# First batch's normalisation split over three engines, key weights split on POOL, and the second projection walked chunk by chunk

## The chip, the cores and the metric

The kernel runs on one core of a Trainium2 chip. Its engines are TensorE (PE), VectorE (DVE), ScalarE (ACT), GpSimd (POOL) and SyncE (SP, which here only issues DMA). Time is the device time of one execution in microseconds; lower is better. Before the change three runs gave a median of 674.53 us (673.94 to 674.96).

## What is computed

Two transformer-like layers on x of shape (2, 512, 512). Only the start matters here: the layer norm of x and the first projections.

```python
xn = _layernorm(x, axis=-1)                 # (x - mean) / sqrt(var + 1e-5), per row of 512
qkv = xn @ w_qkv                            # 512 -> 32 query heads, 8 key heads, 8 value heads of 16
xq, xk = _apply_rope(q), _apply_rope(k)     # products with cos and sin tables, then sums
x = x + attention(xq, xk, xv) @ w_o + ffn0(xn)
xn = _layernorm(x, axis=-1)
x = x + attn1(xn) + ffn1(xn)
```

## The kernel before

Everything is one program with an instruction order written by hand for each engine; semaphores join them. There is no scheduler. The change touches the first stage, `qkv_stage`, which takes about the first 50 us.

The 1024 rows of x are 8 tiles of 128 rows, four for each batch. `Norm` does a tile in steps: `dve_stats` (L88, L90: mean and variance), `act_std` (L94: square root on ACT), `dve_norm` (L98 reciprocal, L100 subtract and multiply, in place), `pe_transpose` (L108, four 128x128 transposes into a bank of PSUM), `act_hi` (L117, rounds the transposed tile to fp32r, the high part) and `dve_lo` (L122, the rest, the low part). Every product is three matmuls, high by high, low by high and high by low (`three_pass`, L52 to L54), so weights are split in the same way: `wqkv_hi` by ACT (L565 for the 128 key columns of all four chunks at once, L577 for the other 640 columns chunk by chunk) and `wqkv_lo` by POOL (L528 keys, L531 chunks 0 to 2) and DVE (L629, chunk 3).

The order on PE: 14 products of the identity matrix (L696) that compute nothing that is kept, the first batch's four tiles with a few more identity products between them (`IDENTITY_PRODUCTS`), then `pair(0)` (keys of the first batch, 12 matmuls), `pair(1)` (24 matmuls), the transposes of the second batch's four tiles (L108 x16), and `pair(2)`. Before `pair(n)` with n of 2 or more PE waits until DVE has made the four rope products (L647) of pair n - 2, because they read the bank that pair n overwrites. So `pair(2)` waits for the products of `pair(0)`.

The order on DVE: the first batch's stats and norms, its four low parts, the second batch's four stats (they wait for the one DMA that loads the second batch), the low part of weight chunk 3, the second batch's four norms, then the products of `pair(0)` and `pair(1)`.

All loads of this stage are issued by SP on one queue, in the order ident, four x tiles, four weight chunks, second batch of x, cos, sin, lr_raw, mask, first feed-forward weights.

## Time and profile before

| | |
|---|---|
| median of three runs | 674.53 us (673.94 to 674.96) |
| the profiled execution, its time | 674.68 us |
| its span in the trace | 672.9 us |
| PE busy | 663.8 us (99%) |
| DVE, ACT, POOL busy | 418.2 (62%), 294.3 (44%), 241.3 us (36%) |

The profiled execution took 1.8 us more than its span, which lies around it. PE is busy in nearly the whole span, so a change can move the end only where PE waits, or where PE does work that could be left out.

### The profile page before, as it was taken

The page shows a single profiled execution, that of the slowest core. Times are in us where ns is not written, and L with a number is a line of the kernel's source. Part 1 is how long each engine was busy: PE and PEld are TensorE (multiplying, and loading weights), DVE is VectorE, ACT ScalarE, POOL GpSimd, SP SyncE. Part 2 cuts the span into 40 slices and gives each one's busy share as a digit, 9 for nine tenths or more (in the row PEclk, how much of TensorE's full clock was granted, in tenths as well). Part 3 has the DMA queues.
Part 4 walks back from the last instruction along what each step waited for, and adds up shares of the span by engine and source line. Part 5 has one row for each costly group of instructions (what it writes and reads, how often), then busy time and mean ns, then how long its engine had stood idle before and what let it go on. Part 6 is the DMA issues. An engine that isn't in the chain of part 4 may idle for free.

```text
span 672.9 us, 9999 instructions
## 1 busy us (share of the span) xinstructions
PE 663.8 (99%) x3518; PEld 505.2 (75%) x3518; DVE 418.2 (62%) x987; ACT 294.3 (44%) x558; POOL 241.3 (36%) x242
## 2 busy tenths in 40 slices
PE   8999999999999999999999999999999999999998
PEld 7786666666666666666787778888888888888886
DVE  6957867766777677665366655377555665646501
ACT  4324555455554555455434425344433444343321
POOL 3595233133222322222234636703232242323443
PEclk9999999999999999999999999999999999999999
DMA  9448334352223322121155520500010011112011
GB/s 292 136 145 185 99 78 109 78 129 78 78 58 89 77 80 65 50 79 49 48 162 161 176 91 1 159 1 32 32 32 33 32 63 32 32 32 78 1 63 62
DMA packets 23145, 55.17 MB, mean 82 GB/s; under 512 B 3732, under 2 KB 4088, under 8 KB 22040
## 3 DMA queue, kind: packets, MB, share of 16 engines
q1 hardware_dynamic: 22840, 54.41, 27.9%
q8 instruction: 28, 0.46, 0.3%
q14 instruction: 21, 0.17, 0.1%
q10 hardware_dynamic: 256, 0.13, 0.1%
HBM read 42.86 MB, written 11.54 MB: 81 GB/s over the span
## 4 chain that ended last, share of the span: by engine, by line
PE 91%; POOL 2%; issue 1%; DVE 1%; DMA 1%; ACT 1%; SPq 1%; ACTq 0%; DVEq 0%
PE bank L52 25%; PE bank L54 23%; PE bank L53 23%; PE bank L1085 6%; PE bank L1120 5%; PE bank L1107 3%; PE bank L180 2%; PE bank L696 1%; PE bank L1093 1%; PE bank L108 1%; PE bank L344 1%; POOL wqkv_lo L531 1%; DMA k_stack<-k_hi 1%; PE bank L1677 1%; DMA q_lo<-rope_lo 1%
## 5 line engine op out<-in xcount | busy, mean ns | idle before, releaser
L1031 DVE CUSTOM_DVE_ANT_0 bank<-bank,mask 128x512 f32<-128x512 f32 (+3 forms) x256 | 118.4, 523 | 57.3 <-PE bank L1085 57.0
L217 POOL TENSOR_TENSOR up_w_lo<-up_w_eff,up_w_hi 128x512 fp32r<-128x512 f32 x50 | 66.8, 1342 | 98.5 <-ACT up_w_hi L213 98.5
L382 POOL TENSOR_TENSOR down_h_lo<-hidden,down_h_hi 128x512 fp32r<-128x512 f32 x50 | 66.2, 1324 | 88.3 <-ACT down_h_hi L377 88.3
L983 ACT ACTIVATE probs<-bank 128x512 f32<-128x512 f32 x160 | 85.0, 598 | 27.6 <-PE bank L1107 24.9
L52 PE MATMUL bank<-x0T_hi,up_w_hi 128*128 128x512 f32 x224 | 95.7, 427 | 0.0
L54 PE MATMUL bank<-x0T_lo,up_w_hi 128*128 128x512 f32 x224 | 88.5, 395 | 0.0
L53 PE MATMUL bank<-x0T_hi,up_w_lo 128*128 128x512 f32 x224 | 88.3, 394 | 0.0
L944 POOL TENSOR_SCALAR_AFFINE_SELECT probs<-probs 128x512 f32<-128x512 f32 x64 | 39.9, 635 | 120.0 <-ACT probs L983 120.0
L52 PE MATMUL bank<-down_w_hi,down_h_hi 128*128 128x512 f32 x200 | 78.5, 392 | 0.4 <-DVE bind_cols L1397 0.4
L53 PE MATMUL bank<-down_w_hi,down_h_lo 128*128 128x512 f32 x200 | 78.0, 390 | 0.0
L377 ACT ACTIVATE down_h_hi<-hidden 128x512 fp32r<-128x512 f32 x50 | 31.6, 631 | 91.3 <-PE bank L54 91.3
L52 PEld LDWEIGHTS bank<-x0T_hi,up_w_hi 128*128 128x128 f32 x224 | 42.0, 187 | 23.4 <-issue 16.5
L1085 PE MATMUL bank<-k_stack,q_stack 48*128 48x512 f32 (+3 forms) x256 | 56.8, 341 | 0.7 <-DMA k_stack<-k_hi 0.7
L1107 PE MATMUL bank<-q_stack,k_stack 49*128 49x512 f32 x160 | 57.0, 443 | 0.0
L284 DVE SCALAR_TENSOR_TENSOR up_gated<-up_tanh,bank 128x512 f32<-128x512 f32 x50 | 34.2, 684 | 32.2 <-ACT up_tanh L277 31.8
L290 DVE SCALAR_TENSOR_TENSOR hidden<-up_gated,bank 128x512 f32<-128x512 f32 x50 | 34.3, 685 | 30.5 <-PE bank L54 30.3
L213 ACT ACTIVATE up_w_hi<-up_w_eff 128x512 fp32r<-128x512 f32 x50 | 31.1, 631 | 47.4 <-DVE up_w_eff L204 47.4
L54 PEld LDWEIGHTS bank<-x0T_lo,up_w_hi 128*128 128x128 f32 x224 | 42.1, 188 | 10.2
L1085 PEld LDWEIGHTS bank<-k_stack,q_stack 48*128 48x128 f32 x256 | 35.7, 185 | 18.1 <-issue 16.3
L53 PEld LDWEIGHTS bank<-x0T_hi,up_w_lo 128*128 128x128 f32 x224 | 42.2, 188 | 6.0
L52 PEld LDWEIGHTS bank<-down_w_hi,down_h_hi 128*128 128x128 f32 x200 | 37.6, 188 | 8.2 <-DVE bind_cols L1397 0.5
L54 PE MATMUL bank<-down_w_lo,down_h_hi 128*128 128x512 f32 x112 | 43.7, 390 | 0.0
(167 smaller groups left out, 1361.2 us busy)
## 6 DMA issues: line engine op xcount, KB each, us to landing
w_raw<-in_w_gate_up SPq DMA_DIRECT2D x25, 512.0 KB, 3.4
w_raw<-in_w_down SPq DMA_DIRECT2D x25, 256.0 KB, 3.6
q_stack<-q_hi SPq DMA_DIRECT2D x32, 128.0 KB, 3.3
att<-att_T SPq DMA_DIRECT2D x16, 256.0 KB, 2.0
q_hi<-rope_hi SPq DMA_DIRECT2D x8, 256.0 KB
q_lo<-rope_lo SPq DMA_DIRECT2D x8, 256.0 KB
q_stack<-q_lo SPq DMA_DIRECT2D x16, 128.0 KB, 3.6
attention_or_xn<-att SPq DMA_DIRECT2D x16, 128.0 KB
```

What stands on the lines that cost most here:

```text
L52: pe.matmul(out, w_hi, m_hi, start=first, stop=False, skip_group_check=True)
L53: pe.matmul(out, w_lo, m_hi, start=False, stop=False, skip_group_check=True)
L54: return pe.matmul(out, w_hi, m_lo, start=False, stop=last, skip_group_check=True)
L217: pool.tensor_tensor(self.half(self.w_lo[:, o % 2], k), self.half(self.w_eff, k), f32(self.half(self.w_hi[:, o % 2], k)), ALU.subtract).th ...
L284: dve.scalar_tensor_tensor(out=self.ut[:, b, :], in0=self.th[:, b, :], scalar=1.0, in1=self.product_bank(o, b, 0)[:, :], op0=ALU.add, op1= ...
L290: dve.scalar_tensor_tensor(out=self.hid[:, o, b * S:(b + 1) * S], in0=self.ut[:, b, :], scalar=0.5, in1=self.product_bank(o, b, 1)[:, :], ...
L382: pool.tensor_tensor(self.h_lo[:, k % 2, :], self.hid[:, o, b * S:(b + 1) * S], f32(self.h_hi[:, k % 2, :]), ALU.subtract).then_inc(self.h ...
L944: pool.affine_select(out=diag, in_=diag, compare_op=ALU.is_ge, fill=0.0, base=0, pattern=[[0, REP], [1, P]], channel_multiplier=-1).then_i ...
L983: act.activation(pt[:, BLOCK_OF[KEY_PIECES[p]], :, :], narrow.bank(("keys", g, p))[:, :].rearrange("p (h s) -> p h s", h=REP), ACT.Exp).th ...
L1031: dve.tensor_tensor_reduce(out=own, in0=own, in1=e.mask[:, S - w:S], scale=1.0, scalar=NEG, op0=ALU.add, op1=ALU.max, accum_out=rmax[:, i, ...
L1085: last = pe.matmul(bank[:, n * w:(n + 1) * w], qst[K, slot, h + n, i * P:(i + 1) * P], kst[K, slot, 0:w], start=(n == 0), stop=(n == nh - ...
L1107: pe.matmul(narrow.bank(("keys", g, p))[:, :], kst[K, slot, j * P:(j + 1) * P], qst[K, slot, :, i * P:(i + 1) * P], start=True, stop=True) ...
```

## The change

1. Loads: ident is issued by ACT, ahead of its other work, instead of by SP. The key columns of all weights come as one DMA (256 KB in rows of 512 bytes), the other 640 columns as four. cos and sin are issued ahead of the second batch of x.
2. The first batch's norm: tile 0 by POOL, tiles 1 and 3 by ACT (as x * rstd + shift, where DVE makes the 128x1 shift = -mean * rstd), tile 2 by DVE.
3. Key weights: POOL makes both high and low part; ACT's L565 goes away.
4. DVE does the low part of weight chunk 3 ahead of the second batch's stats instead of behind them.
5. `pair(1)` goes chunk by chunk over both its halves, instead of half by half.
6. Identity products: 10 instead of 14 at the start, and 2, 2, 2, 5 behind the tiles instead of 2, 3, 2, 7.

```diff
         def sync(sp):
-            sp.dma_start(e.ident[:, :], d["ident"]).then_inc(e.ident_in, 16)
             for t in range(NJ):
                 sp.dma_start(x_sb[:, t, :], d["x"][t * P:(t + 1) * P, :]).then_inc(x_loaded[t], 16)
+            sp.dma_start(w_raw[:, :, 0:P], d["w_qkv"][:, 0:P].rearrange("(c p) n -> p c n", p=P)).then_inc(w_loaded[0], 16)
             for c in range(NC):
-                sp.dma_start(w_raw[:, c, :], d["w_qkv"][c * P:(c + 1) * P, :]).then_inc(w_loaded[c], 16)
-            sp.dma_start(x_sb[:, NJ:, :], d["x"][S:].rearrange("(t p) n -> p t n", p=P)).then_inc(x_loaded[NJ], 16)
+                sp.dma_start(w_raw[:, c, P:], d["w_qkv"][c * P:(c + 1) * P, P:]).then_inc(w_loaded[1], 16)
             sp.dma_start(cos[:, :], d["cos"]).then_inc(consts, 16)
             sp.dma_start(sin[:, :], d["sin"]).then_inc(consts, 16)
+            sp.dma_start(x_sb[:, NJ:, :], d["x"][S:].rearrange("(t p) n -> p t n", p=P)).then_inc(x_loaded[NJ], 16)
...
-            pool.wait_ge(w_hi_ready, 1)
-            pool.tensor_tensor(w_lo[:, :, 0:P], w_raw[:, :, 0:P], f32(w_hi[:, :, 0:P]), ALU.subtract).then_inc(w_lo_ready, 1)
+            pool.wait_ge(norm.rst, 1)
+            pool.tensor_scalar(x_sb[:, 0, :], x_sb[:, 0, :], norm.mv[:, 0, 0:1], norm.rstd[:, 0:1],
+                               ALU.subtract, ALU.mult).then_inc(by_pool, 1)
+            pool.wait_ge(w_loaded[0], 16)
+            pool.tensor_copy(w_hi[:, :, 0:P], w_raw[:, :, 0:P]).then_inc(by_pool, 1)
+            pool.wait_ge(by_pool, 2)
+            pool.tensor_tensor(w_lo[:, :, 0:P], w_raw[:, :, 0:P], f32(w_hi[:, :, 0:P]), ALU.subtract).then_inc(by_pool, 1)
...
+            def normalise(t):
+                act.wait_ge(shifted, 1 + t // 2)
+                act.activation(x_sb[:, t, :], x_sb[:, t, :], ACT.Identity, bias=shift[:, t:t + 1],
+                               scale=norm.rstd[:, t:t + 1]).then_inc(act_normed, 1)
+
+            act.dma_start(e.ident[:, :], d["ident"]).then_inc(e.ident_in, 16)
             norm.act_std(act, 0)
             norm.act_std(act, 1)
             norm.act_std(act, 2)
+            normalise(1)
+            norm.act_std(act, 3)
             norm.act_hi(act, 0)
-            norm.act_std(act, 3)
+            normalise(3)
             norm.act_hi(act, 1)
             norm.act_hi(act, 2)
-            split_keys()
             norm.act_hi(act, 3)
+            act.wait_ge(w_loaded[1], 16 * NC)
             for c in range(NC):
                 act.activation(w_hi[:, c, P:], w_raw[:, c, P:], ACT.Copy).then_inc(w_hi_ready, 1)
...
             for t in range(NJ):
                 norm.dve_lo(dve, t)
+            dve.wait_ge(w_hi_ready, NC)
+            dve.tensor_tensor(w_lo[:, NC - 1, P:], w_raw[:, NC - 1, P:], f32(w_hi[:, NC - 1, P:]), ALU.subtract).then_inc(w_lo_last, 1)
             for t in range(NJ, NT):
                 norm.dve_stats(dve, t)
-            dve.wait_ge(w_hi_ready, NC + 1)
-            dve.tensor_tensor(w_lo[:, NC - 1, P:], w_raw[:, NC - 1, P:], f32(w_hi[:, NC - 1, P:]), ALU.subtract).then_inc(w_lo_last, 1)
...
-                for r in range(1 if k == 0 else 2):
+                halves = range(1 if k == 0 else 2)
+                for c, r in ((c, r) for c in range(NC) for r in halves) if n == 1 else ((c, r) for r in halves for c in range(NC)):
...
-            identity_products(14)
+            identity_products(10)
```

On DVE, the piece between the first batch's low parts (L122) and the products of pair 0 (L647 before, L673 now). Before:

```order
L122 TENSOR_TENSOR x0T_lo<-bank,x0T_hi 128x4x128 x4
L88 BN_STATS norm_stats<-x 128x6
L90 BN_AGGR norm_mv<-norm_stats 128x2
...
L629 TENSOR_TENSOR wqkv_lo<-wqkv_raw,wqkv_hi 128x640
L98 RECIPROCAL norm_rstd<-norm_std 128x1
L100 TENSOR_SCALAR x<-x,norm_mv,norm_rstd 128x512
```

And now:

```order
L122 TENSOR_TENSOR x0T_lo<-bank,x0T_hi 128x4x128 x4
L653 TENSOR_TENSOR wqkv_lo<-wqkv_raw,wqkv_hi 128x640
L88 BN_STATS norm_stats<-x 128x6
L90 BN_AGGR norm_mv<-norm_stats 128x2
...
L98 RECIPROCAL norm_rstd<-norm_std 128x1
L100 TENSOR_SCALAR x<-x,norm_mv,norm_rstd 128x512
```

The weight chunk moved from behind the second batch's four stats to ahead of them; the stats, norms and products behind it are the same instructions in the same order.

On SP, the queue of loads at the start of the program. Before:

```order
L487 DMA ident<-in_ident 128x128
L489 DMA x<-in_x 128x512 x4
L491 DMA wqkv_raw<-in_w_qkv 128x768 x4
L492 DMA x<-in_x 128x4x512
L493 DMA cos<-in_cos 128x512
L494 DMA sin<-in_sin 128x512
L495 DMA lr_raw<-in_lr 96x4096
```

And now:

```order
L492 DMA x<-in_x 128x512 x4
L493 DMA wqkv_raw<-in_w_qkv 128x4x128
L495 DMA wqkv_raw<-in_w_qkv 128x640 x4
L496 DMA cos<-in_cos 128x512
L497 DMA sin<-in_sin 128x512
L498 DMA x<-in_x 128x4x512
L499 DMA lr_raw<-in_lr 96x4096
```

The second batch of x (128x4x512) is now the last load ahead of lr_raw, where sin was; ident has left this queue.

## Rows read from the trace of the kernel before

**Rows 1.** Waits of PE, whole span: us in total, times, longest.
```profile
PE bank L1085 <- DMA k_stack<-k_hi: 0.7, 1, 0.7
```

**Rows 2.** Timeline of DVE, 4 to 24.4: start us, us, instruction, idle before.
```profile
5.92 0.13 DVE L98 RECIPROCAL norm_rstd<-norm_std 128x1 f32<-128x1 f32 x1
...
14.42 0.69 DVE L88 BATCH_NORM_STATS2 norm_stats<-x 128x6 f32<-128x512 f32 x1 [0.81 <-DMA x<-in_x]
...
17.63 1.38 DVE L629 TENSOR_TENSOR wqkv_lo<-wqkv_raw,wqkv_hi 128x640 fp32r<-128x640 f32 x1
18.93 0.15 DVE L98 RECIPROCAL norm_rstd<-norm_std 128x1 f32<-128x1 f32 x1
...
21.55 0.67 DVE L647 SCALAR_TENSOR_TENSOR rope_products<-bank,cos 64x512 f32<-64x512 f32 x1
...
23.69 0.69 DVE L647 SCALAR_TENSOR_TENSOR rope_products<-bank,cos 64x512 f32<-64x512 f32 x1
```

**Rows 3.** Timeline of PE, 12.6 to 24.6.
```profile
13.89 0.47 PE L52 MATMUL bank<-x0T_hi,wqkv_hi 128*128 128x512 f32 x1 [0.20 <-POOL wqkv_lo L528]
...
22.69 1.91 PE L108 MATMUL bank<-ident,x 128*128 128x128 f32 x16
24.44 0.49 PE L52 MATMUL bank<-x0T_hi,wqkv_hi 128*128 128x512 f32 x1
```

**Rows 4.** Timeline of SP, 0 to 9.2: its DMA issues.
```profile
0.81 0.39 SPq L487 DMA_DIRECT2D ident<-in_ident  x1
...
5.04 0.81 SPq L492 DMA_DIRECT2D x<-in_x  x1
...
7.11 0.44 SPq L494 DMA_DIRECT2D sin<-in_sin  x1
```

**Rows 5.** DMA by short windows: size, us from issue to landing; packets moved, 2.0 to 2.5.
```profile
DMA packets 104, 0.06 MB, mean 112 GB/s; under 512 B 16, under 2 KB 97, under 8 KB 104
...
wqkv_raw<-in_w_qkv SPq DMA_DIRECT2D x1, 384.0 KB, 6.7
...
x<-in_x SPq DMA_DIRECT2D x1, 1024.0 KB, 9.4
...
sin<-in_sin SPq DMA_DIRECT2D x1, 256.0 KB, 9.5
```

**Rows 6.** Timeline of ACT, 4 to 19.
```profile
12.29 0.59 ACT L117 ACTIVATE x0T_hi<-bank 128x512 fp32r<-128x512 f32 x1
12.77 2.61 ACT L577 ACTIVATE wqkv_hi<-wqkv_raw 128x640 fp32r<-128x640 f32 x4
```

**Rows 7.** Timeline of POOL, 0.7 to 19.
```profile
12.47 1.27 POOL L528 TENSOR_TENSOR wqkv_lo<-wqkv_raw,wqkv_hi 128x512 fp32r<-128x512 f32 x1 [9.83 <-ACT wqkv_hi L565]
13.71 4.62 POOL L531 TENSOR_TENSOR wqkv_lo<-wqkv_raw,wqkv_hi 128x640 fp32r<-128x640 f32 x3
```

**Rows 8.** Timelines of POOL and DVE, 46 to 52.
```profile
46.22 2.56 POOL L217 TENSOR_TENSOR up_w_lo<-up_w_eff,up_w_hi 128x512 fp32r<-128x512 f32 x2
48.73 2.28 POOL L547 TENSOR_TENSOR rope_sum<-rope_products 128x512 f32<-128x512 f32 x1
...
47.65 2.21 DVE L638 TENSOR_TENSOR rope_lo<-rope_sum,rope_hi 128x1024 fp32r<-128x1024 f32 x1
```

**Rows 9.** Groups of POOL by form: busy us, mean ns, idle before.
```profile
L944 POOL TENSOR_SCALAR_AFFINE_SELECT probs<-probs 128x512 f32<-128x512 f32 x64 | 39.9, 635 | 120.0 <-ACT probs L983 120.0
```

**Rows 10.** Timeline of PE, 2 to 12 (x4 is one tile's transposes).
```profile
2.68 6.13 PE L696 MATMUL bank<-ident 128*128 128x128 f32 x28 [2.68 <-DMA ident<-in_ident]
8.65 0.60 PE L108 MATMUL bank<-ident,x 128*128 128x128 f32 x4
...
9.54 0.60 PE L108 MATMUL bank<-ident,x 128*128 128x128 f32 x4
...
11.53 0.60 PE L108 MATMUL bank<-ident,x 128*128 128x128 f32 x4
```

**Rows 11.** Windows at the end: PE busy first, PEclk is the granted clock.
```profile
669.00:672.90 3.90, 0.73 (x4) 0.27 (x2) 1.45 (x3) 0.00 (x0) 0.00 (x0) 1.00 0.73 269
```

More of the change, by code:

```diff
@@ L465, in qkv_stage @@
                     e.xT_hi, e.xT_lo)
-        w_loaded = [sem(f"wqkv_loaded{c}") for c in range(NC)]
+        w_loaded = [sem("wqkv_keys_loaded"), sem("wqkv_rest_loaded")]
         consts = sem("rope_tables_loaded")
@@ L469, in qkv_stage @@
         lr_lo, products, stored = e.lr0_lo, e.rope_products, e.rope_stored
-        w_hi_ready, w_lo_ready, w_lo_last = sem("wqkv_hi_ready"), sem("wqkv_lo_ready"), sem("wqkv_lo_last_ready")
+        shift = sb("norm_shift", [P, NJ])
+        shifted, act_normed, by_pool = sem("norm_shift_ready"), sem("normed_by_act"), sem("tile0_normed_keys_hi_keys_lo_wqkv_lo")
+        norm.normed_in_order = {0: (by_pool, 1), 1: (act_normed, 1), 3: (act_normed, 2),
+                                **{t: (norm.normed, t - 2) for t in range(NJ, NT)}, 2: (norm.normed, 1)}
+        w_hi_ready, w_lo_last = sem("wqkv_hi_ready"), sem("wqkv_lo_last_ready")
         v_mm, v_rows, v_ones = sem("v_mm"), sem("v_rows_copied"), sem("v_ones")
@@ L561, in scalar @@
         def scalar(act):
-            def split_keys():
-                for c in range(NC):
-                    act.wait_ge(w_loaded[c], 16)
-                act.activation(w_hi[:, :, 0:P], w_raw[:, :, 0:P], ACT.Copy).then_inc(w_hi_ready, 1)
+            def normalise(t):
[3 more added lines that the diff above has]
+            act.dma_start(e.ident[:, :], d["ident"]).then_inc(e.ident_in, 16)
             norm.act_std(act, 0)
@@ L618, in vector, with reciprocal, shift_of @@
         def vector(dve):
-            norm.dve_stats(dve, 0)
-            for t in range(1, NJ):
-                norm.dve_stats(dve, t)
-                norm.dve_norm(dve, t - 1)
-            norm.dve_norm(dve, NJ - 1)
+            def reciprocal(t):
+                dve.wait_ge(norm.stdd, t + 1)
+                dve.reciprocal(norm.rstd[:, t:t + 1], norm.std[:, t:t + 1]).then_inc(norm.rst, 1)
+            def shift_of(t):
+                dve.wait_ge(norm.rst, t + 1)
+                dve.tensor_scalar(shift[:, t:t + 1], norm.mv[:, t, 0:1], norm.rstd[:, t:t + 1], -1.0,
+                                  ALU.mult, ALU.mult).then_inc(shifted, 1)
+            norm.dve_stats(dve, 0)
+            norm.dve_stats(dve, 1)
+            reciprocal(0)
+            norm.dve_stats(dve, 2)
+            reciprocal(1)
+            shift_of(1)
+            norm.dve_stats(dve, 3)
+            norm.dve_norm(dve, 2)
+            reciprocal(3)
+            shift_of(3)
             for t in range(NJ):
                 norm.dve_lo(dve, t)
+            dve.wait_ge(w_hi_ready, NC)
+            dve.tensor_tensor(w_lo[:, NC - 1, P:], w_raw[:, NC - 1, P:], f32(w_hi[:, NC - 1, P:]), ALU.subtract).then_inc(w_lo_last, 1)
             for t in range(NJ, NT):
                 norm.dve_stats(dve, t)
-            dve.wait_ge(w_hi_ready, NC + 1)
-            dve.tensor_tensor(w_lo[:, NC - 1, P:], w_raw[:, NC - 1, P:], f32(w_hi[:, NC - 1, P:]), ALU.subtract).then_inc(w_lo_last, 1)
             for t in range(NJ, NT):
```

27 lines of the change are left out of this document (13 added, 14 removed).

## The prediction

> **What bounds the kernel now.** PE is busy in 99% of the span (table above), so I first read PE's waits over the whole span: behind the start, no wait on a load or a store is longer than 0.7 us [rows 1]. A time won or lost in the first stage, at the point where PE goes over to unbroken work, should then reach the end whole, because everything behind hangs on PE's own order. That point is `pair(2)`. So the question is when PE can start it, and I read the timelines of the engines up to there.
>
> PE starts `pair(0)` at 13.89, its second-batch transposes at 22.69 and `pair(2)` at 24.44 [rows 3]. The transposes, 16 of them and two records each, end their issue at about 24.4. DVE ends the fourth product of `pair(0)`, for which `pair(2)` waits, at 23.69 + 0.69 = 24.38 [rows 2]. The two paths arrive together: no wait shows, but DVE's path has no slack at all. This is the thing to see before any sum is made: a faster PE alone wins nothing here.
>
> DVE's path begins at 14.42, when the second batch of x has landed: stats to 17.63, the low part of weight chunk 3 to 18.93, norms to 21.55, products to 24.38 [rows 2]. Without the weight chunk that is 3.21 + 5.45 = 8.66 us from the first stats to the end of the fourth product.
>
> **PE's side, part by part.** The 14 identity products and the tile behind them are spaced (8.65 - 2.68) / 28 = 0.213 us a record; behind that a tile with its two identity products, 8 records, takes 9.54 - 8.65 = 0.89 us, 0.11 a record [rows 10]. That is the lower and the higher of the two clock levels (1.2 and 2.4 GHz), and the rise came at the end of this unbroken work. With ten products, tile 0 can be transposed at 2.68 + 20 x 0.213 = 6.94, tile 1 at 6.94 + 8 x 0.213 = 8.65 (still the lower level), tiles 2 and 3 at 9.54 and 10.43, ended at 11.03. Before, tile 3 started at 11.53 [rows 10] and its high part on ACT, behind the key weights, at 12.29 [rows 6]. Now ACT can start it at 11.06, 1.23 earlier. `pair(0)` came 13.89 - 12.29 = 1.60 behind it and should come at 12.66.
>
> For this the four norms must be ready in time. POOL's tensor_scalar is not in the trace of before. The nearest row with one input is 0.635 us for 128x512 [rows 9], one with two inputs 1.27 [rows 7]; I take the first, for the kind, and both are covered: the reciprocal of tile 0 ended at 5.92 + 0.13 = 6.05 before [rows 2] and should end near 5.7, with ident's 0.39 of issue gone from SP's queue [rows 4]; so POOL is done at 6.4 to 7.0 against 6.94. ACT's normalisation I price by its 128x512 pass, 0.59 [rows 6]: two of them, and both stand where ACT waited for PE. DVE loses three norms of 0.55 and gains two 128x1 operations; it is not late there. POOL's copy and subtraction for the keys, 0.6 to 1.3 plus 1.27, end near 10 and are hidden until 12.66.
>
> `pair(0)` and `pair(1)` are 36 matmuls at 0.233, 8.4 us, if nothing stops them. Before they took 22.69 - 13.89 = 8.8, as PE waited 0.4 for POOL's third chunk. The new order asks for chunk 2 only after 12 matmuls of `pair(1)`, near 18.3, and POOL has it by 17.7 (below). So PE is through at 21.1 instead of 22.69, 1.6 us earlier. If PE alone counted, this would be the gain.
>
> **DVE's side.** ACT starts the high parts of the other weights 12.77 - 12.29 = 0.48 behind tile 3 [rows 6], now at 11.54, and ends them 2.61 later, at 14.15. The last weight load, issued some 0.47 ahead of the 5.04 of the next, landed 6.7 later, at 11.27 [rows 4, 5], so this holds if it is no later. DVE then asks for the low part of chunk 3 at 14.2. POOL is at its own three chunks by then, 4.62 / 3 = 1.54 each [rows 7], at 12.3 to 13.9, to 15.4, to 16.95. Here the rows show a clash. Before, DVE's L629 took 1.38 from 17.63 [rows 2] while POOL's last chunk ran until 18.33 [rows 7]; 19.01 - 18.33 leaves 0.68 for the work itself. Again DVE's L638, asked at 47.65, ended at 49.86, 1.13 behind the end of POOL's second L217 at 48.73, and POOL's next instruction took 2.28 instead of 1.27 [rows 8]. Two-input work in SBUF on the two engines takes turns by instruction. So DVE does chunk 3 at 15.4 to 16.1, and POOL's third chunk is 0.7 later, at 17.65. DVE's next step can't start before 16.07.
>
> The Trainium skill has this as a rule (SBUF — State Buffer, Who interferes with whom): a DVE instruction with two SBUF inputs and a GpSimd instruction that reads SBUF share one port pair, and the second blocks until the first has ended. By that rule the trace agrees; without it the bound would be 14.2 + 0.7 = 14.9.
>
> Then the load. The second batch of x landed at 5.04 + 9.4 = 14.44, with cos and sin behind it; sin landed at 7.11 + 9.5 = 16.61 [rows 4, 5]. Now cos and sin are ahead, and the second batch stands where sin stood, with the same bytes in front of it. It should land when sin did, 16.61, less about 0.3 since ident (0.39 of issue [rows 4]) runs beside the queue, plus about 0.25 for the key columns in 512-byte rows. That last number is my choice between nothing and 2 us: from 2.0 to 2.5 us, where ident's small rows moved, the queue made 112 GB/s, at which 256 KB would take 2.3 us [rows 5], but that stretch is mostly the start of the first transfer. I take 16.55.
>
> DVE's stats start at the later of 16.07 and 16.55. The products of `pair(0)` end at 16.55 + 8.66 = 25.21, and `pair(2)` starts at 25.27 instead of 24.44. The last norm ends at 22.5, so the transposes are over by 23.0 and PE then stands still for over 2 us. The 1.6 us won on PE are given back in that wait, and 0.83 more is lost.
>
> **Sum.** Pair 2 later by 0.83, the rest unchanged in order and length: by the profiled execution 674.68 + 0.83 = 675.5; the median of the runs shown is 0.15 lower, so 675.4 for the median. All edits on PE, POOL and ACT are worth nothing of their own here; their cover is DVE's path, and if that were gone they would give 1.6.
>
> **Rivals.**
> - *The load isn't late.* cos and sin are a quarter of the bytes of this stretch, and sin may have been slow through lr_raw's large rows beside it. Between the last weights (11.27) and the second batch (14.44) the queue moved 1 MB in 3.17 us [rows 5]; by that rate 512 KB more put the second batch 1.58 later, less 0.05 as above, at 15.97. Then DVE's turn behind POOL decides (16.07): 24.73 + 0.06, +0.35, or +0.2 to -0.3 if the turns fall better. 674.2 to 674.9. 17 in 100.
> - *PE decides after all*: DVE's path is short enough, and the gain is the 1.6 to 1.75 us of PE: 672.8 to 673.0. It needs stats at 14.9 or earlier. Against it: DVE can't have chunk 3 before ACT's 14.15, and the 8.66 us behind. 5 in 100.
> - *Small rows cost more*: the queue behind the key columns is 0.6 to 2 us later. Over 0.5 more, the loss passes 1.35; 676.0 to 677.5. 8 in 100.
> - *POOL isn't ready for early work.* Before, POOL did nothing for 9.83 us ahead of its first arithmetic at 12.47 [rows 7], so nothing shows that it could work at 5.7. If it starts only at t, PE waits at tile 0 for t + 0.64, and as it is idle from 6.94, it is likely at its lower clock again behind. From t = 7 on, each us comes into ACT's 11.54 and from there into DVE's. For a price I take t = 9, halfway between 5.7 and 12.47: tile 0 at 9.65, 2.7 later than in my sum, the weights' high parts at 14.2, DVE's stats 4.5 behind them at 18.7, `pair(2)` at 27.4: +3.0, 677.5; with a low clock for all four tiles up to 679. 15 in 100.
> - *The clock falls in PE's 2 us wait.* At the lower level a matmul takes 0.2 us more, and some 8 of them cost 1.7: 677. Against it: in the last 3.9 us PE did 0.73 us of work and the granted clock stayed 1.00 [rows 11]. 5 in 100.
>
> The GPSIMD Engine Reference of the Trainium skill (2.1, Instruction dispatch) says that the first call of a freshly loaded GpSimd kernel also pays for loading its code, about 6 us. Counted from the end of POOL's memsets at 12.47 - 9.83 = 2.64 that would be a start at 8.6 and 677.1, an estimate by that page. No run here shows it.
>
> **How the numbers follow.** My forecast has the remaining 50 in 100, 675.4, its own range 674.9 to 675.9. About 0.2%, 1.35 us, is what a measurement of this kernel can tell from no change. Faster: only the PE rival, 0.05. Slower: small rows, POOL and clock, 0.28. Same: 0.67. The range leaves out the PE rival below, and the worse half of POOL's and of the clock's above: 673.9 to 677.1.
>
> **What would show it.** Right: the first stats of the second batch start at 16 to 17 us; PE starts `pair(0)` near 12.7, ends `pair(1)` near 21, and waits over 1.5 us for DVE's products ahead of `pair(2)` at 25.3; DVE's weight chunk (L653) takes over 1.2 us, with POOL's end as its releaser in time; POOL's tensor_scalar starts near 5.7. Wrong: stats at 15, or `pair(2)` right behind the transposes; a POOL instruction that starts at 8 or later, with PE idle from 7. What makes the prediction wrong most easily is the landing of the second batch, on which the whole sum hangs one for one.

## The result and the profile after

The changed kernel takes 676.83 us (median of 14 executions, 675.25 to 678.49), the kernel before 674.74 us in the same comparison (14 executions, 673.94 to 675.89). The ratio is 1.003, with a 95% interval of 1.0019 to 1.004: slower, by 2.1 us or 0.3%. The forecast was 675.4 us, in a range of 673.9 to 677.1.

The 14 times of the changed kernel don't lie around their median. They fall into two groups, and the mean granted clock of PE over the whole span, which is kept for each execution, parts them exactly:

| mean granted clock | executions | times |
|---|---|---|
| 0.999 to 1.000 | 7 | 675.25 to 676.23, median 675.77 |
| 0.997 | 7 | 677.42 to 678.49, median 677.72 |

The forecast of 675.4 is close to the first group. The second group is 1.95 us longer, all of it lies above the top of the range (677.1), and the profiled execution (677.42 us, span 675.7 us) is one of it. All 78 executions of the kernel before that stood beside the experiments have 0.999 or 1.000. One of these 78 took 677.45 us all the same, so a long time alone is no sign of a lower clock.

The page of the profiled execution, parts 1 and 2, shows this only in one digit. PE is still busy in 98% of the span, and the clock has an 8 in the second of the 40 slices (16.9 to 33.8 us), where the page of the kernel before has a 9:

```profile
PE 663.2 (98%) x3504; PEld 505.0 (75%) x3504; DVE 417.7 (62%) x986; ACT 295.4 (44%) x559; POOL 244.7 (36%) x244
...
PEclk9899999999999999999999999999999999999999
```

The waits of PE in this execution (us in total, times, longest) show a new one, 1.9 us for DVE's products, and the first one, for ident, was 2.68 us before [rows 10]. The last line is the longest wait of the kernel before behind the start:

```profile
PE bank L722 <- DMA ident<-in_ident: 3.9, 1, 3.9
PE bank L52 <- DVE rope_products L673: 1.9, 1, 1.9
...
PE bank L1093 <- DVE minus_max L1041: 0.8, 1, 0.8
```

The timeline of DVE from 14.9 to 25.6 (start us, us, instruction, idle before) is the path that `pair(2)` waits for, where [rows 2] showed the old one:

```profile
15.07 1.95 DVE L653 TENSOR_TENSOR wqkv_lo<-wqkv_raw,wqkv_hi 128x640 fp32r<-128x640 f32 x1 [1.81 <-ACT wqkv_hi L589]
16.95 0.68 DVE L88 BATCH_NORM_STATS2 norm_stats<-x 128x6 f32<-128x512 f32 x1
...
22.74 0.68 DVE L673 SCALAR_TENSOR_TENSOR rope_products<-bank,cos 64x512 f32<-64x512 f32 x1
...
24.88 0.69 DVE L673 SCALAR_TENSOR_TENSOR rope_products<-bank,cos 64x512 f32<-64x512 f32 x1
```

The stats start at 16.95, and 24.88 + 0.69 = 25.57 is 8.62 behind that: the 8.66 of the forecast. No wait for a load shows in front of the stats. POOL's timeline from 5 to 19 has the norm of tile 0 at 2.08 us, where the cast behind it, over as many elements, takes 0.61:

```profile
5.61 2.08 POOL L532 TENSOR_SCALAR x<-x,norm_mv,norm_rstd 128x512 f32<-128x512 f32 x1 [2.98 <-DVE norm_rstd L633]
7.64 0.61 POOL L535 CAST wqkv_hi<-wqkv_raw 128x512 fp32r<-128x512 f32 x1
...
13.23 5.22 POOL L540 TENSOR_TENSOR wqkv_lo<-wqkv_raw,wqkv_hi 128x640 fp32r<-128x640 f32 x3 [3.58 <-ACT wqkv_hi L589]
```

In two narrow windows of the same engine the second and the third of those three stand alone:

```profile
14.77 1.56 POOL L540 TENSOR_TENSOR wqkv_lo<-wqkv_raw,wqkv_hi 128x640 fp32r<-128x640 f32 x1
...
16.30 2.15 POOL L540 TENSOR_TENSOR wqkv_lo<-wqkv_raw,wqkv_hi 128x640 fp32r<-128x640 f32 x1
```

DVE asked for its chunk at 15.07 and got its turn only when POOL's second was over, at 14.77 + 1.56 = 16.33; POOL's third then waited for DVE's.

PE's timeline from 2 to 13.6 and from 21 to 31:

```profile
3.95 4.63 PE L722 MATMUL bank<-ident 128*128 128x128 f32 x20 [3.95 <-DMA ident<-in_ident]
8.38 0.87 PE L108 MATMUL bank<-ident,x 128*128 128x128 f32 x4
...
13.31 0.50 PE L52 MATMUL bank<-x0T_hi,wqkv_hi 128*128 128x512 f32 x1 [0.30 <-DVE x0T_lo L122]
...
21.58 0.39 PE L54 MATMUL bank<-x0T_lo,wqkv_hi 128*128 128x512 f32 x1
21.82 1.91 PE L108 MATMUL bank<-ident,x 128*128 128x128 f32 x16
25.63 0.51 PE L52 MATMUL bank<-x0T_hi,wqkv_hi 128*128 128x512 f32 x1 [1.91 <-DVE rope_products L673]
...
27.21 0.63 PE L53 MATMUL bank<-x0T_hi,wqkv_lo 128*128 128x512 f32 x1
27.64 0.63 PE L54 MATMUL bank<-x0T_lo,wqkv_hi 128*128 128x512 f32 x1
...
30.32 0.40 PE L53 MATMUL bank<-x0T_hi,wqkv_lo 128*128 128x512 f32 x1
30.56 0.39 PE L54 MATMUL bank<-x0T_lo,wqkv_hi 128*128 128x512 f32 x1
```

`pair(2)` starts at 25.63 and its early matmuls follow each other by 0.43 us, later ones by 0.24. The windows around it (from:to, length, then PE, PEld, DVE, ACT, POOL busy, the granted clock, the DMA share and GB/s) say why:

```profile
23.75:25.63 1.88, 0.00 (x1) 0.00 (x1) 1.79 (x4) 0.83 (x2) 0.00 (x0) 1.00 0.10 33
25.63:27.00 1.37, 1.37 (x4) 1.14 (x5) 1.37 (x3) 0.00 (x0) 1.35 (x2) 0.63 0.00 0
27.00:28.00 1.00, 1.00 (x3) 0.78 (x3) 1.00 (x2) 0.00 (x0) 1.00 (x1) 0.50 0.00 0
28.00:29.00 1.00, 1.00 (x4) 0.74 (x3) 1.00 (x3) 0.79 (x1) 1.00 (x2) 0.50 0.00 0
29.00:30.00 1.00, 1.00 (x5) 0.81 (x4) 1.00 (x3) 1.00 (x2) 1.00 (x2) 0.80 0.00 0
```

PE stood still for 1.9 us at full clock. Some 0.4 us after it had started again the grant fell to 0.50, the lower level (1.2 GHz), and it came back at 29.4.

The granted clock says nothing of this kind about the start. The ten products and tile 0 run at 0.22 us a record, about half the pace of what follows, but the grant of that stretch is 1.00:

```profile
3.95:8.38 4.43, 4.43 (x21) 4.43 (x22) 3.97 (x13) 1.63 (x5) 2.69 (x3) 1.00 1.02 355
```

So the slower pace at the start is read from the spacing of the records alone. It is the pace of the lower level: transposes follow each other by 0.21 us in e9 where the grant is 0.50 (below). But it is in no granted clock, and an execution with a late start does not stand out by its mean clock. "The pace rose" is said below of such a start.

**The account of this execution.** Before, `pair(2)` started at 24.44 and the rest took 674.68 - 24.44 = 650.24 us [rows 3]. Now it starts at 25.63, 1.19 later, and the rest takes 677.42 - 25.63 = 651.79, 1.55 more. The sum is the 2.74 us between the two profiled executions.

### The profile page after: what moved, and what is told of

Same layout as the page of the kernel before. It is cut to its first block, busy times and chain, and to the rows that moved or that the text cites. A ratio compares the mean times of both kernels' runs of the same rounds, so it can differ in the third digit from the quotient of the medians.

```text
span 675.7 us, 9972 instructions
## 1 busy us (share of the span) xinstructions
PE 663.2 (98%) x3504; PEld 505.0 (75%) x3504; DVE 417.7 (62%) x986; ACT 295.4 (44%) x559; POOL 244.7 (36%) x244
## 3 DMA queue, kind: packets, MB, share of 16 engines
HBM read 42.86 MB, written 11.54 MB: 81 GB/s over the span
## 4 chain that ended last, share of the span: by engine, by line
PE 90%; DVE 3%; ACT 2%; DMA 2%; issue 2%; POOL 1%; SPq 1%; ACTq 0%; DVEq 0%
PE bank L52 25%; PE bank L54 23%; PE bank L53 23%; PE bank L1111 6%; PE bank L1146 5%; PE bank L1133 3%; PE bank L180 2%; PE bank L1119 1%; PE bank L722 1%; PE bank L344 1%; PE bank L108 1%; DMA k_stack<-k_hi 1%; PE bank L1703 1%; DMA q_lo<-rope_lo 1%; DMA ident<-in_ident 0%
## 5 line engine op out<-in xcount | busy, mean ns | idle before, releaser
L284 DVE SCALAR_TENSOR_TENSOR up_gated<-up_tanh,bank 128x512 f32<-128x512 f32 x50 | 34.2, 684 | 31.9 <-ACT up_tanh L277 31.8
```

Of the source, the lines that this page charges most:

```text
L284: dve.scalar_tensor_tensor(out=self.ut[:, b, :], in0=self.th[:, b, :], scalar=1.0, in1=self.product_bank(o, b, 0)[:, :], op0=ALU.add, op1= ...
```

## The experiments

Twelve kernels in three sets of four. The letters in the expectations are the theories as each expectation gives them; A is in most of them the theory that stood at the end: the wait of `pair(2)` for DVE's path, which the low part of weight chunk 3 lengthens by a turn behind POOL, and in some executions the fallen clock behind PE's standstill. In this table "rest" is the time of the profiled execution less the start of `pair(2)`, "still" is how long PE stood ahead of `pair(2)`, and "fell" is how many of all executions have a mean granted clock under 0.998.

| kernel | median us | ratio to before (95%) | profiled | `pair(2)` | rest | still | fell |
|---|---|---|---|---|---|---|---|
| before | 674.74 | | 674.68 | 24.44 | 650.24 | 0 | 0 of 78 |
| changed | 676.83 | 1.003 (1.0019 to 1.004) | 677.42 | 25.63 | 651.79 | 1.9 | 7 of 14 |
| e1_fill | 676.14 | 1.0021 (1.0011 to 1.0031) | 676.92 | 26.47 | 650.45 | filled | 0 of 12 |
| e2_w3_pool | 675.26 | 1.0005 (0.9997 to 1.0014) | 675.33 | 25.02 | 650.31 | 2.0 | 0 of 11 |
| e3_ident_sp | 677.24 | 1.0034 (1.0022 to 1.0045) | 677.34 | 27.21 | 650.13 | 1.9 | 3 of 7 |
| e4_before_w3 | 676.27 | 1.002 (1.0011 to 1.0029) | 676.32 | 25.91 | 650.41 | 0.9 | 0 of 10 |
| e5_w3_pool_x2 | 674.10 | 1.0000 (0.9992 to 1.0009) | 673.99 | 23.60 | 650.39 | 0.3 | 0 of 11 |
| e6_tile0_dve | 673.98 | 0.9994 (0.9985 to 1.0003) | 676.96 | 25.80 | 651.16 | 1.9 | 1 of 12 |
| e7_w3_behind | 676.87 | 1.0038 (1.0025 to 1.0051) | 677.88 | 26.18 | 651.70 | 2.0 | 2 of 6 |
| e8_x2_first | 675.87 | 1.0031 (1.002 to 1.0043) | 675.82 | 25.22 | 650.60 | 1.9 | 2 of 7 |
| e9_long_wait | 680.15 | 1.0081 (1.0064 to 1.0098) | 680.15 | 28.11 | 652.04 | 1.8, 1.6 | 5 of 5 |
| e10_long_wait_fill | 678.72 | 1.006 (1.0045 to 1.0075) | 677.96 | 27.84 | 650.12 | filled | 0 of 6 |
| e11_no_pool_norm | 673.87 | 0.9989 (0.998 to 0.9997) | 674.06 | 24.00 | 650.06 | 0 | 0 of 12 |
| e12_act_norms | 673.54 | 0.9984 (0.9974 to 0.9995) | 673.64 | 23.65 | 649.99 | 0 | 0 of 12 |

The table carries the main finding. In the ten profiled executions without a fall the rest takes 649.99 to 650.60 us, whatever stands in front, so in these executions all of a kernel's loss or gain is in the start of `pair(2)`. In the four with one it takes 651.16 to 652.04. The median of before was 674.89 beside the first four, 674.41 beside the next and 674.52 beside the last, so medians of different sets are best compared by their distance from it (+2.1 for the changed kernel). `pair(2)` and all that is read from a timeline is of one execution of each kernel.

**e4_before_w3: one part of the change alone.** The kernel before, with the low part of weight chunk 3 moved ahead of the second batch's stats on DVE.

```diff
-            for t in range(NJ, NT):
-                norm.dve_stats(dve, t)
             dve.wait_ge(w_hi_ready, NC + 1)
             dve.tensor_tensor(w_lo[:, NC - 1, P:], w_raw[:, NC - 1, P:], f32(w_hi[:, NC - 1, P:]), ALU.subtract).then_inc(w_lo_last, 1)
             for t in range(NJ, NT):
+                norm.dve_stats(dve, t)
+            for t in range(NJ, NT):
                 norm.dve_norm(dve, t)
```

> The kernel before with one part of the change alone: the low part of weight chunk 3 on DVE ahead of the second batch's stats. Theory A, this move with POOL's turn is what makes DVE's path longer: DVE asks at 15.4, gets its turn behind POOL's second chunk (16.8) and ends at 17.5; stats at 17.45 instead of 14.42, pair(2) at 26.1, +1.7, and PE stands still for over 1 us, so part of the runs may show the clock falling for +1.7 more: median 676.4 to 678. Theory B, the move is harmless: within 0.3 of before.

DVE's timeline from 13 to 20 has the same clash as the changed kernel's:

```profile
15.25 2.05 DVE L627 TENSOR_TENSOR wqkv_lo<-wqkv_raw,wqkv_hi 128x640 fp32r<-128x640 f32 x1 [1.82 <-ACT wqkv_hi L577]
17.23 0.68 DVE L88 BATCH_NORM_STATS2 norm_stats<-x 128x6 f32<-128x512 f32 x1
```

The second batch's stats move from 14.42 [rows 2] to 17.23, `pair(2)` from 24.44 to 25.91, and the time rises by 0.2%, as theory A has it; of its falls of the clock none came, with a standstill of 0.9 us. This part alone, without another order of loads, without POOL's new work and without ident's move, costs 1.4 us in the median (676.27 against 674.89), no less than the changed kernel loses in its executions without a fall (675.77 against 674.74).

**e2_w3_pool: that part taken out of the changed kernel.** POOL does chunk 3 too, as its fourth.

```diff
-            for c in range(NC - 1):
+            for c in range(NC):
                 pool.wait_ge(w_hi_ready, c + 1)
...
-            dve.wait_ge(w_hi_ready, NC)
-            dve.tensor_tensor(w_lo[:, NC - 1, P:], w_raw[:, NC - 1, P:], f32(w_hi[:, NC - 1, P:]), ALU.subtract).then_inc(w_lo_last, 1)
```

> The changed kernel with the low part of weight chunk 3 made by POOL as a fourth chunk; DVE goes from the first batch's low parts straight to the second batch's stats. Theory A, DVE's path from the turn behind POOL (stats at 16.95) decides: stats now start when the load lands, at 15.4, pair(2) at 15.4 + 8.66 = 24.1 or, if PE's transposes are last, near 24.2; PE waits under 0.8 us, the clock stays; 674.3, that is -0.4 against before. POOL's fourth chunk ends near 19.5, ahead of the 20.4 at which PE asks. Theory B, the load decides or moves later with it: stats at 16.5 or later, 675.8 or more.

DVE, from 15 to 17.3, now waits for the load, which came 0.9 us later in this execution than in the changed kernel's (16.33 against 15.42):

```profile
16.33 0.70 DVE L88 BATCH_NORM_STATS2 norm_stats<-x 128x6 f32<-128x512 f32 x1 [3.78 <-DMA x<-in_x]
```

The stats win only 16.95 - 16.33 = 0.62 us, `pair(2)` 0.61; with the load at 15.42 they would have won 1.5, an estimate from the two timelines. The outcome lies between the two theories: the load decided, as in B, but landed before its 16.5. PE still stood for 2.0 us, yet in 11 executions the clock never fell; the median, 675.26, is 0.5 under that of the changed kernel's upper clock group (675.77).

**e7_w3_behind: chunk 3 back behind the stats.** Only those lines of the change are undone; the load stays behind cos and sin.

```diff
-            dve.wait_ge(w_hi_ready, NC)
-            dve.tensor_tensor(w_lo[:, NC - 1, P:], w_raw[:, NC - 1, P:], f32(w_hi[:, NC - 1, P:]), ALU.subtract).then_inc(w_lo_last, 1)
             for t in range(NJ, NT):
                 norm.dve_stats(dve, t)
+            dve.wait_ge(w_hi_ready, NC)
+            dve.tensor_tensor(w_lo[:, NC - 1, P:], w_raw[:, NC - 1, P:], f32(w_hi[:, NC - 1, P:]), ALU.subtract).then_inc(w_lo_last, 1)
```

> The changed kernel with one part undone: DVE's low part of weight chunk 3 stands behind the second batch's stats again. Theory A (the turn behind POOL costs only when DVE gets there early): stats start as the load lands, 15.1 to 16.6, chunk 3's 0.7 to 1.4 follows with POOL's last chunk nearly over, pair(2) at 15.8 + 8.66 + 0.7 = 25.2 on average; 675.5, that is 1.2 under the changed kernel. Theory B (the order makes no difference as the sum of DVE's work is the same): 676.8.

This was missed: 675.5 was expected and the median is 676.87. The second batch landed at 16.76 in this execution, so the chunk's 0.79 us came on top of a late load instead of being hidden in front of it. DVE, 14 to 22:

```profile
16.76 0.69 DVE L88 BATCH_NORM_STATS2 norm_stats<-x 128x6 f32<-128x512 f32 x1 [3.11 <-DMA x<-in_x]
...
19.97 0.79 DVE L655 TENSOR_TENSOR wqkv_lo<-wqkv_raw,wqkv_hi 128x640 fp32r<-128x640 f32 x1
```

That adds up to `pair(2)` (16.76 + 8.62 + 0.79 = 26.17). The profile does not show the chunk to be as dear behind the stats as ahead of them: with the changed kernel's landing, 15.42, the same sum gives 24.83, an estimate, against 25.63. The four executions without a fall have 675.35 to 677.22, median 676.15, too few and too wide to tell the two orders apart.

**e8_x2_first: the load early again, the chunk ahead.** The second batch is issued ahead of cos and sin, as before.

```diff
+            sp.dma_start(x_sb[:, NJ:, :], d["x"][S:].rearrange("(t p) n -> p t n", p=P)).then_inc(x_loaded[NJ], 16)
             sp.dma_start(cos[:, :], d["cos"]).then_inc(consts, 16)
             sp.dma_start(sin[:, :], d["sin"]).then_inc(consts, 16)
-            sp.dma_start(x_sb[:, NJ:, :], d["x"][S:].rearrange("(t p) n -> p t n", p=P)).then_inc(x_loaded[NJ], 16)
```

> The changed kernel with one part undone: the second batch of x loaded ahead of cos and sin again. Theory A: the stats wait for the turn behind POOL, near 16.95, and not for the load, so that an earlier load changes nothing where it landed by 16.9 anyway: 676.8, within 0.5 of the changed kernel. Theory B (the load is late in most runs, as in my forecast): 0.5 to 1 less, 676.

DVE, 14 to 18, again with the turn behind POOL and no load in front of the stats:

```profile
14.67 1.95 DVE L653 TENSOR_TENSOR wqkv_lo<-wqkv_raw,wqkv_hi 128x640 fp32r<-128x640 f32 x1 [1.81 <-ACT wqkv_hi L589]
16.54 0.68 DVE L88 BATCH_NORM_STATS2 norm_stats<-x 128x6 f32<-128x512 f32 x1
```

Without a fall its executions have a median of 675.82, against 675.77 of the changed kernel. The median of all seven, 675.87, is what theory B gave (676), but the profile has theory A's mechanism, and the number hangs on how many executions fall. An earlier load shows no gain as long as the chunk stands in front; the 0.41 us by which `pair(2)` is earlier in this profile came with DVE's asking 0.40 earlier, out of the front.

**e5_w3_pool_x2: both out.** The diffs of e2 and e8 together.

> The changed kernel with weight chunk 3's low part on POOL and the second batch of x loaded ahead of cos and sin, as before. Theory A (time = start of pair(2) + 650.3, and that start is the last of DVE's path from the load and PE's own path): the load lands near 14.6 instead of 15.1 to 16.6, pair(2) by DVE at 14.6 + 8.7 = 23.3, PE's own path ends at 22.9 to 23.4; 673.6 to 674.0 in the median, faster than before by 1. Theory B (the load is not on the path): as with the fourth chunk on POOL alone, 675.2.

DVE from 13 to 26:

```profile
13.84 0.69 DVE L88 BATCH_NORM_STATS2 norm_stats<-x 128x6 f32<-128x512 f32 x1 [0.96 <-DMA x<-in_x]
...
17.21 0.56 DVE L100 TENSOR_SCALAR x<-x,norm_mv,norm_rstd 128x512 f32<-128x512 f32 x1
...
17.88 1.60 DVE L100 TENSOR_SCALAR x<-x,norm_mv,norm_rstd 128x512 f32<-128x512 f32 x1
```

POOL's fourth chunk, in a narrow window:

```profile
17.45 1.74 POOL L540 TENSOR_TENSOR wqkv_lo<-wqkv_raw,wqkv_hi 128x640 fp32r<-128x640 f32 x1
```

And PE from 21 to 24.5:

```profile
21.43 1.91 PE L108 MATMUL bank<-ident,x 128*128 128x128 f32 x16
23.60 0.51 PE L52 MATMUL bank<-x0T_hi,wqkv_hi 128*128 128x512 f32 x1 [0.26 <-DVE rope_products L671]
```

The stats are at 13.84, 3.1 us earlier than in the changed kernel, `pair(2)` is at 23.60, 2.0 earlier, and the median falls from 676.83 to 674.10, or from 2.1 above the kernel before to 0.3 under it. The two terms hide each other: e2 alone gave 0.6 us of `pair(2)`, e8 alone 0.4 (and that from the front), and both give 2.0. The load's own spread blurs the single figures. With the order of the changed kernel it landed at 15.07 to 16.75 (issue plus time to landing, seven kernels), with the old order at 13.75 to 14.44 in six kernels and at 17.08 in e6.

A norm of one tensor input took 1.60 instead of 0.55 beside POOL's fourth chunk, so that clash isn't one of two-input work alone. It isn't a whole turn either: the norm ended at 19.48, 0.29 behind POOL's 19.19, which is less than its own 0.55. The stats, from 13.84 on beside POOL's chunks, kept their 0.66 to 0.69.

**e1_fill: the standstill filled.** The changed kernel with eight products of the identity ahead of `pair(2)`, into a bank that is free.

```diff
                 norm.pe_transpose(pe, t, t - NJ)
+            identity_products(8, 1)
             pair(2)
```

> The changed kernel with 8 identity products (into a bank that nobody reads) between the second batch's transposes and pair(2), where PE stood still for 1.9 us. They compute nothing that is kept. Theory A, the standstill lets TensorE's clock fall: DVE's path is as before, pair(2) still starts near 25.6, but no stretch at granted clock 0.5 behind it; the runs lose their upper group (677.4 to 678.5) and all lie near 675.3 to 676.3, that is +1.0 against before. Theory B, the clock falls for another reason (fewer products at the start, the later first matmul): half of the runs stay near 677.7, the median near 676.8. Theory C, the products delay pair(2): over 676.8.

In none of 12 executions did the clock fall (7 of 14 without the fill). The median is 0.7 us lower, and the intervals of the two ratios overlap. Theory A wanted all executions between 675.3 and 676.3; six of the 12 lie above, up to 678.47, at a granted clock of 1.000. So a second source of spread is left. The profiled execution, 676.92, shows one such source, the start. PE, 7 to 14.3:

```profile
8.75 1.06 PE L108 MATMUL bank<-ident,x 128*128 128x128 f32 x4
...
10.38 0.60 PE L108 MATMUL bank<-ident,x 128*128 128x128 f32 x4
...
14.16 0.50 PE L52 MATMUL bank<-x0T_hi,wqkv_hi 128*128 128x512 f32 x1 [0.29 <-DVE x0T_lo L122]
```

Here the distance from tile 0 to tile 1 is 1.63 us; at the faster pace it is 0.89 [rows 10], and in the changed kernel's profile 9.53 - 8.38 = 1.15. The pace rose later, which is 0.48, and ident landed later (PE started at 4.33, not 3.95), which is 0.37. `pair(0)` came 0.85 later than 13.31, the sum of the two, and `pair(2)`, at 26.47, as much (0.84). In e2 the same distance was 0.88 and `pair(0)` at 12.60. Whether the same two make the executions of 677.79 and 678.47 is not shown; neither was profiled.

**e3_ident_sp: ident back on SP's queue.**

```diff
         def sync(sp):
+            sp.dma_start(e.ident[:, :], d["ident"]).then_inc(e.ident_in, 16)
...
-            act.dma_start(e.ident[:, :], d["ident"]).then_inc(e.ident_in, 16)
```

> The changed kernel with ident issued by SP ahead of x, as before. Theory A, ident on ACT's queue is late by 1.3 us (3.95 instead of 2.68) and starts PE late: PE starts at 2.7, has its ten products at 6.9, then waits for POOL's norm of tile 0 (7.7 to 8.1, as x lands 0.4 later); tile 0's transposes start at 8.1 instead of 8.16, so nothing is won: POOL's 2.08 us norm takes the place; the time as the changed kernel or up to 0.5 worse through the lower clock. Theory B, PE's start was what made the front late: weights' high parts on ACT 0.5 to 1 us earlier (12.43 to 11.5..11.9), pair(2) at 24.7 to 25.1, -0.5 to -1 against the changed kernel.

PE started at 2.7, as it did before, but this bought nothing (1.0034 against 1.003). PE, 7 to 14.3:

```profile
8.19 1.11 PE L108 MATMUL bank<-ident,x 128*128 128x128 f32 x4 [0.84 <-POOL x L533]
...
9.95 1.06 PE L108 MATMUL bank<-ident,x 128*128 128x128 f32 x4
```

PE was through its ten products early, stood 0.84 us for POOL's 2 us norm, and kept the slower pace up to the third tile (9.95 - 8.19 = 1.76 from the first to the second). `pair(0)` came at 14.90, 1.59 later than in the changed kernel. There the late landing of ident had covered POOL's dear norm. This is one execution: the seven run from 675.58 to 678.26, and those with a fall (676.98, 677.37, 678.26) and without one (675.58 to 677.34) overlap, so something besides the fall spreads this kernel as much as the fall does.

**e6_tile0_dve: tile 0 on DVE, tile 2 on POOL**, with ident on SP and e5's two edits.

```diff
-            pool.wait_ge(norm.rst, 1)
-            pool.tensor_scalar(x_sb[:, 0, :], x_sb[:, 0, :], norm.mv[:, 0, 0:1], norm.rstd[:, 0:1],
+            pool.wait_ge(norm.rst, 3)
+            pool.tensor_scalar(x_sb[:, 2, :], x_sb[:, 2, :], norm.mv[:, 2, 0:1], norm.rstd[:, 2:3],
                                ALU.subtract, ALU.mult).then_inc(by_pool, 1)
...
-            reciprocal(0)
+            norm.dve_norm(dve, 0)
...
+            reciprocal(2)
...
-            norm.dve_norm(dve, 2)
```

> As the kernel with chunk 3 on POOL and the second batch ahead, and besides tile 0 normalised by DVE and tile 2 by POOL, and ident issued by SP. Theory A (the head of PE's path is ident's late landing on ACT's queue and POOL's 2.08 us norm of tile 0): PE starts at 2.7, tile 0's transposes at 6.9 to 7.0, pair(0) at 12.3 to 12.7, PE never idle between; PE is ready for pair(2) at 22.5 to 22.9, DVE's path at 23.3 decides: 673.6, and with a narrower spread than the changed kernel's as the clock rises in unbroken work. Theory B (POOL's long norm hurts wherever it stands): tile 2 is ready at 9.2 or later and the front is no earlier, pair(0) at 13.3, 674.0 or more.

The median, 673.98, is that of theory B (674.0 or more) rather than the 673.6 of theory A: PE started early but waited 0.86 us for ACT's norm of tile 1 and 0.37 for POOL's of tile 2, and `pair(0)` came at 13.44. POOL's timeline, 8 to 12, shows that the 2.08 us does not hang on which tile it is or when it runs:

```profile
8.36 2.08 POOL L533 TENSOR_SCALAR x<-x,norm_mv,norm_rstd 128x512 f32<-128x512 f32 x1 [5.73 <-DVE norm_rstd L633]
```

Its profile is the one execution of 12 with a fall: the second batch landed at 17.11 there, and PE stood for 1.9 us. The other eleven have a median of 673.95.

**e9_long_wait and e10_long_wait_fill: the clock by itself.** e9 is the changed kernel with four repeated stats on DVE, written to a spare tile, so that PE stands twice: 1.8 us ahead of the second batch's transposes and 1.6 behind them. e10 is e9 with 21 identity products in PE's gaps.

```diff
+            for t in range(NJ, NT):
+                dve.bn_stats(extra[:, :], x_sb[:, t, :]).then_inc(again, 1)
+                dve.wait_ge(again, t - NJ + 1)
...
             pair(1)
+            identity_products(8, 1)
             for t in range(NJ, NT):
                 norm.pe_transpose(pe, t, t - NJ)
+                identity_products(1, 1)
+            identity_products(9, 1)
             pair(2)
```

(The first block is in both, the second in e10 alone.)

> The changed kernel with the second batch's four first statistics instructions done once more by DVE into a spare tile (not used), so that DVE's path is some 2.9 us longer and PE has less to do ahead of pair(2). Theory A (time = start of pair(2) + 650.3, and a standstill of PE there lets the clock fall by chance, the more surely the longer it is): pair(2) near 28.5, the clock at 0.5 for 3.4 us behind it in most runs, 678.8 without and 680.3 to 680.8 with the fall; median near 680.5. Theory B (the fall has nothing to do with PE's standstill): half of the runs at 678.8, half at 680.5, or none.

> The same with 21 identity products into a bank that nobody reads, spread over the time in which PE would stand still there. Theory A: pair(2) starts at the same time (28.5), no stretch at granted clock 0.5 behind the start, all runs near 678.8 up to the spread of the clock's rise at the start; 1.5 or more under the kernel without them. Theory B: no difference, or slower by the products.

Windows of e9 (columns as above):

```profile
25.00:28.00 3.00, 1.48 (x8) 0.83 (x6) 2.91 (x5) 1.53 (x3) 0.00 (x0) 0.51 0.00 0
28.00:32.00 4.00, 3.89 (x9) 3.10 (x10) 3.97 (x8) 1.32 (x2) 3.87 (x4) 0.51 0.00 0
```

The same windows of e10:

```profile
25.00:28.00 3.00, 3.00 (x28) 2.96 (x28) 2.88 (x6) 1.28 (x3) 0.13 (x1) 1.00 0.06 23
28.00:32.00 4.00, 4.00 (x18) 3.23 (x19) 4.00 (x7) 1.55 (x2) 4.00 (x4) 1.00 0.01 2
```

From 28 to 32 both wait for nothing to speak of; PE does 9 matmuls in e9 and 18 in e10. In e9 the grant fell at 25.1, in the middle of the transposes and so behind the first gap of 1.8 us, and was back at 31.9. Its last transposes, at 0.50, start at 25.84 and 26.05, the spacing of the start of the program:

```profile
25.84 0.63 PE L108 MATMUL bank<-ident,x 128*128 128x128 f32 x2
26.05 0.42 PE L108 MATMUL bank<-ident,x 128*128 128x128 f32 x1
```

The clock fell in 5 of 5 executions without the fill and in 0 of 6 with it. More work on PE made the program 1.43 us faster (680.15 to 678.72); of the six times with the fill only one is above the lowest of the five without it.

**e11_no_pool_norm and e12_act_norms: what a better version needs.** e11 is e5 with ident on SP and no norm on POOL: tiles 0 and 2 on DVE, 1 and 3 on ACT, whose norm of tile 1 comes ahead of the root of tile 2. e12 also gives ACT the norms of tiles 5 and 7 of the second batch, which takes two of them out of DVE's path. The diff is that of e12 against e11.

```diff
             for t in range(NJ, NT):
                 norm.dve_stats(dve, t)
-            for t in range(NJ, NT):
+            for t in range(NJ, NT, 2):
                 norm.dve_norm(dve, t)
+                reciprocal(t + 1)
+                shift_of(t + 1)
...
                 norm.act_std(act, t)
+            normalise(5)
+            normalise(7)
```

> Chunk 3 on POOL, second batch ahead of cos and sin, ident on SP, tiles 0 and 2 normalised by DVE and 1 and 3 by ACT, none by POOL, ACT's norm of tile 1 ahead of the root of tile 2. Theory A (PE's head is freed of ident's late landing and POOL's 2.08 us): tile 0 transposed at 6.9, pair(0) at 12.5 to 13.2, PE unbroken until then; pair(2) at 23.0 to 23.5; 673.5 in the median, 0.9 under before. Theory B (the front has no more to give, since weights' landing at 11.2 decides): 674.0 as with POOL's norm.

> As the kernel without POOL's norm, and besides tiles 5 and 7 of the second batch normalised by ACT (idle there), which takes 0.6 us from DVE's path. Theory A (DVE's path from the load still decides by some tenths): pair(2) 0.3 to 0.6 earlier, 673.1. Theory B (PE's own path, end of pair(1) + 1.75, decides): no change against the kernel without POOL's norm.

PE in e12, 6.3 to 14 (first row) and 21 to 24.5:

```profile
9.92 0.66 PE L108 MATMUL bank<-ident,x 128*128 128x128 f32 x4 [1.02 <-DVE x L100]
...
21.99 1.91 PE L108 MATMUL bank<-ident,x 128*128 128x128 f32 x16
23.65 0.48 PE L52 MATMUL bank<-x0T_hi,wqkv_hi 128*128 128x512 f32 x1
```

Nothing is left between the transposes and `pair(2)`. e12 is 0.16% faster than before (0.9984, interval 0.9974 to 0.9995), e11 0.11%; their intervals overlap, so ACT's two norms are seen in `pair(2)` (24.00 to 23.65) but not for certain in the time. Both medians are 0.4 us above what theory A gave (673.5 and 673.1); in the profiles `pair(0)` came at 13.56 and 13.49, where 12.5 to 13.2 was expected of e11. The profiled executions differ by 1.04 us (674.68 to 673.64), of which 0.79 is the start of `pair(2)` (24.44 to 23.65). PE's own path is the bound here, and in it PE waits 1.02 us at 9.92 for the norm of tile 2, made by DVE, which is what would be next.

## Why the prediction was right, and where

**The number: inside the range by luck.** The median rose by 2.1 us, where 0.9 was forecast from the three times of before. By the prediction's own limit of 1.35 us that is "slower", to which it gave 0.28, against 0.67 for "same". Seven of the 14 executions lie above the top of the range; with an eighth among them the median would have been near 677.4 and out of it.

**The place and the chain: right, and shown.** The start of `pair(2)` carries the result one for one (rest 649.99 to 650.60 in ten kernels, the one before included), PE's earlier end of `pair(1)` is given back in a standstill, and DVE's path from the first stats is 8.62 us against 8.66. The forecast for `pair(2)` was 25.27; it started at 25.63. Of the signs that were named, the stats (16.95), the wait (1.9), L653's 1.95 and POOL's start (5.61) came true; `pair(0)` at 13.31 and the end of `pair(1)` at 21.82 are 0.6 and 0.7 late. One reading was a slip: the 16 transposes are one record each, not two, as their x16 says; the end of their issue, about 24.4, stands.

**"The later of 16.07 and 16.55": the terms changed places.** The step had the turn behind POOL at 16.07 and the load at 16.55, and let the load decide. In the profiled execution the turn decided, at 16.95, and the load had landed first: SP issued it at 6.32, and it took 9.1 us, 15.42. The load isn't a fixed term: by DVE's waits in other kernels with the same order of loads it landed at 16.33 (e2) and 16.76 (e7). 16.55 lies among these, but not in this execution: the load was 1.1 too late in the forecast and the turn 0.9 too early, and that the two errors left the start of the stats within 0.4 is luck. Each term alone is nearly enough for the loss, as e2 and e8 (0.6 and 0.4 us won) show against e5 (2.0 us); e4 shows it of the turn with nothing else changed.

**The turn was 0.9 us late, by two terms of the front.** ident "beside the queue" was priced as free: PE was to start at 2.68 as before, and started at 3.95, since ident landed 3.1 us after its issue on ACT's queue. The records up to tile 0 took 4.43 instead of 4.26. Against that the pace rose earlier in PE's work than assumed (tile 1 was 1.15 behind tile 0, where 1.71 was put in), which gave back 0.6. So `pair(0)` came at 13.31, not 12.66, and ACT's high parts at 12.43, not 11.54. DVE asked at 15.07, not 14.2. Its turn cost 1.95 - 0.68 = 1.27, about what the step had (16.1 - 14.2 less 0.7 is 1.2).

**POOL's norm: 2.08 us, not "0.635 to 1.27".** Both rows taken for the bounds were other operations, and the price lay above both. It cost nothing in this profile only because ident was late too (the norm ended at 7.69, PE was at tile 0 at 8.38); with that cover gone PE waited 0.84 us for it in e3. The median does not show it.

**"If that were gone they would give 1.6": not seen.** With DVE's path shortened as far as here, in e12, `pair(2)` came 0.79 us earlier than before and the median 1.0, from a kernel whose norms were dealt out anew as well. PE's side had lost part of the 1.6 to waits ahead of `pair(0)`, 1.02 us for a norm in e12 among them. What the new order of `pair(1)`, the split of the key weights and the fewer identity products give, each by itself, was not tried.

**Rival "POOL isn't ready for early work": refuted.** Its norm began at 5.61, right behind DVE's reciprocal. The GPSIMD Engine Reference of the Trainium skill (2.1, Instruction dispatch), by which the first call would be some 6 us late, isn't borne out for these operations; in e11 POOL's first arithmetic is the cast, and it took 0.61 at once. Whether they need code that has to be loaded first no run shows.

**Rival "the clock falls": given 5 in 100, and true in 7 of 14.** The argument against it was that near the end of the span the grant stayed 1.00 with little work on PE [rows 11]. That stretch says nothing of what the grant does when work comes back behind a standstill, since no work came back. It should have been read as no evidence. The price, 1.7 us, was good: 1.55 in the profile, 1.95 between the groups. Its "some 8 matmuls" stood on no row; in the profile about nine are slow. This rival is why the result is 1.4 us above the forecast, and nearly the whole difference: the executions without it have 675.77, against 675.4.

**The rival "small rows cost more"** has little to show for it: the load was earlier than forecast in this execution, and with the key columns in small rows and the old order behind them it landed at 13.75 to 13.86 in four kernels, against 14.44 and 14.14 without them. The 17.08 of e6 has the same rows and stays unexplained.

## What to carry to other kernels

Find the wait at which the bounding engine goes over to unbroken work, and ask what its releaser's path has in slack before adding up what the bounding engine saves. Two causes that end at the same wait hide each other, so undoing one shows little (0.6 and 0.4 us here) and undoing both shows all (2.0). And a wait on PE isn't only its own length: look at the granted clock of each execution, not only of the profiled one, and where a standstill can't be taken away, products that compute nothing in it kept the clock up here (0 of 12 and 0 of 6).
